# Two last stages of a transformer kernel: attention's work spread over its steps, and mixture-of-experts in one block with rounded output products

## What is computed

```python
h = layernorm(x) * (1 + ca) + sa
x = x + ga * attention(h)       # 16 heads of 64, all 1024 keys, scores + rel_bias[j - i]
h = layernorm(x) * (1 + cb) + sb
logits = h @ gate_w             # 8 experts
top_w = softmax(two largest logits);  cw = top_w at their experts, 0 elsewhere
for e in range(8):
    out += cw[:, e:e+1] * (gelu(h @ w1[e] + b1[e]) @ w2[e] + b2[e])   # 128 -> 512 -> 128
x = x + gb * out
```

## Time and profile before

| | us |
|---|---|
| median of 3 runs (2817.11 to 2831.84) | 2823.53 |
| the profiled execution | 2821.27 |
| its span, first to last instruction | 2819.3 |

### The profile page before, as it was taken

One profiled execution on the slowest core, in us unless ns is written; L12 is line 12 of the kernel. 1 busy time (PEld: TensorE's weight loads), 2 busy tenths in 40 slices (PEclk: granted clock), 3 DMA queues, 4 the chain that ended last, 5 costly groups with the idle time before them and its releaser, 6 DMA issues. The chain is left out here.

```text
span 2819.3 us, 119352 instructions
## 1 busy us (share of the span) xinstructions
PE 2504.6 (89%) x52916; PEld 2026.4 (72%) x53012; DVE 2073.4 (74%) x2409; ACT 1931.1 (68%) x3809; POOL 1455.5 (52%) x1016
## 2 busy tenths in 40 slices
PE   4469999999999999999999998589999999986998
PEld 2157877777888788787878887366676676765887
DVE  5378888778888888887878885489888888973112
ACT  2367888788888888888888876566666666643443
POOL 0188887778788878877888774112122121211000
PEclk8689999999999999999999999799999999997999
DMA  0223433333333333333433332122223132210000
GB/s 33 61 68 91 98 95 83 83 94 84 95 92 96 83 94 88 100 79 91 98 88 77 90 77 53 44 48 59 61 47 71 38 70 59 47 34 16 16 22 30
DMA packets 274599, 193.96 MB, mean 69 GB/s; under 512 B 117545, under 2 KB 215857, under 8 KB 273969
## 3 DMA queue, kind: packets, MB, share of 16 engines
q1 hardware_dynamic: 274096, 186.49, 27.3%
HBM read 29.10 MB, written 1.05 MB: 11 GB/s over the span
## 5 line engine op out<-in xcount | busy, mean ns | idle before, releaser
L728 POOL TENSOR_TENSOR lt_t_sin<-lt_qk,lt_tab 128x512 f32<-128x512 f32 x384 | 685.6, 1807 | 263.1 <-DVE lt_qk L1097 260.6
L733 POOL TENSOR_TENSOR lt_qr<-lt_qr,lt_t_sin 128x1024 f32<-128x1024 f32 x192 | 455.5, 2372 | 27.9 <-POOL lt_t_sin L728 0.5
L1631 DVE TENSOR_REDUCE fa_neg_max<-bank 128x1 f32<-128x1024 f32 x256 | 301.2, 1218 | 91.2 <-PE bank L1458 90.9
L1090 DVE TENSOR_REDUCE lt_ssq<-lt_qr 128x32 f32<-128x2048 f32 x96 | 219.5, 2286 | 155.6 <-ACT lt_qr L962 155.6
L788 PE MATMUL bank<-lt_w_high,lt_x_high 128*128 128x512 f32 x576 | 281.2, 488 | 33.8 <-POOL lt_w_low L696 29.0
L1571 ACT ACTIVATE fa_prob<-bank,fa_neg_max 128x1024 f32<-128x1024 f32 x128 | 142.5, 1113 | 243.7 <-DVE fa_neg_max L1631 127.0
L1641 DVE STREAM_TRANSPOSE fa_prob_t<-fa_prob 128x1024 f32<-128x1024 f32 x256 | 301.8, 1218 | 0.0
L1481 PE MATMUL bank<-fa_prob_t,fa_v 32*64 32x128 f32 x16384 | 276.8, 274 | 23.7 <-issue 17.9
L1481 PEld LDWEIGHTS bank<-fa_prob_t,fa_v 32*64 32x64 f32 x16384 | 240.4, 130 | 71.5 <-issue 43.2
L805 PE MATMUL bank<-ident,lt_qr 128*128 128x128 f32 x1536 | 234.5, 276 | 32.3 <-POOL lt_qr L733 15.9
L1097 DVE TENSOR_TENSOR lt_qk<-lt_qk,lt_rn 128x2048 f32<-128x2048 f32 x96 | 233.0, 2427 | 31.9 <-ACT lt_rn L975 30.7
(11 more groups left out here) (226 smaller groups left out, 5707.1 us busy)
## 6 DMA issues: line engine op xcount, KB each, us to landing
lt_v<-lt_v_tok SPq DMA_DIRECT2D x576, 128.0 KB
fa_v<-fa_v_tok SPq DMA_DIRECT2D x256, 128.0 KB, 3.1
lt_v<-lt_v_tok SPq DMA_DIRECT2D x192, 64.0 KB
lt_k_t<-lt_k_t SPq DMA_DIRECT2D x84, 128.0 KB, 2.6
lt_v<-lt_v SPq DMA_DIRECT2D x168, 64.0 KB, 2.0
lt_w_raw<-in_lt_wqkv_dram SPq DMA_DIRECT2D x36, 256.0 KB, 3.8
lt_x_s<-h_in SPq DMA_DIRECT2D x96, 64.0 KB, 2.7
lt_f_x<-h_mid SPq DMA_DIRECT2D x96, 64.0 KB, 2.1
```

Of the source, the lines that this page charges most:

```text
L728: pool.tensor_tensor(dst[:, :, i, :], src[:, :, 1 - i, :], tab[:, g // 2 % 2, 1, at:at + 32].unsqueeze(1).to_broadcast([P, HEADS, 32]), AL ...
L733: pool.tensor_tensor(qr[:, g % 2, half], qr[:, g % 2, half], t_sin[:, :], ALU.add).then_inc(S.rotated, 1)
L1631: dve.tensor_reduce(neg_max[:, u % 2, par:par + 1], bank[:, 2 * par:2 * par + 2, :].rearrange("p a n -> p (a n)"), AX.X, ALU.max, negate=T ...
```

## The change

In `full_attention`: the jobs come two at a time, at s=0, 2 and 3 (their banks are renumbered). The result of a quad is copied by ScalarE (`att`) at s=3, and Gpsimd multiplies it by the inverses (`divide`), where VectorE did both. The bias band is split by ScalarE (`round_rel`) and Gpsimd (`split_rel`) into `rel_high` and `rel_low`, `anti` is rounded once, and four rounded matmuls take the place of two full ones. `load_rel` waits for the remainder of the pair before. Each DMA of `place_v` waits for a further exponential.

In `experts`: one block without a loop holds all. `down` has the hidden features of the result on partitions and 512 tokens in the row, and is made in three rounded products from `w2_high`, `w2_low`, `hid_high` and `hid_low`. ScalarE rounds hidden blocks 0 and 2, VectorE 1 and 3, and VectorE makes all differences. The routing weights are turned by PE (`turn_weights`, banks 6 and 7), copied by ScalarE behind the Gelus of the second chunk, stored as 8 rows to HBM (`cw_kept`) and read back, one row per expert over all partitions (`spread_weights`, 1 MB each). `weigh` adds the bias (a column of the transposed `b2`), multiplies, and adds to `acc`, for 512 tokens at once. PE takes the logits and the transpose of `b2` first, then `up(0)`; VectorE takes the remainders of `h`, the routing, and then the hidden blocks. Weights of expert e are loaded once expert e-2 has passed its Gelus, and split behind the second chunk of expert e-1. At the end VectorE multiplies by `gb` and adds `x_main` for each chunk, PE turns it (`turn_out`, four full float32 transposes), ScalarE copies it out, SP stores it.

```diff
--- before.py
+++ after.py
...
         def jobs_at(u):
             q, s = u // UPQ, u % UPQ
             half = q // QPH + 1
-            if s % 2 == 1 or half >= HALVES:
+            if s == 1 or half >= HALVES:
                 return []
-            first = JPH * half + 6 * (q % QPH)
-            return list(range(first, first + 4) if s == 0 else range(first + 4, first + 6))
+            first = JPH * half + 6 * (q % QPH) + max(0, 2 * (s - 1))
+            return [first, first + 1]
...
                         for a in range(4):
+                            exponents = 3 * (QB * half - 1) + 4 * i + a
+                            if exponents > 0:
+                                sp.wait_ge(S.probs, exponents)
...
+                def divide(q):
+                    pool.wait_ge(S.att, q + 1)
+                    if q >= 2:
+                        pool.wait_ge(S.out, 2 * (q - 1))
+                    pool.tensor_tensor(att_t[:, q % 2, :].rearrange("p (u a r) -> p a u r", u=UPQ, a=4),
+                                       att[:, :, :].rearrange("p a (u r) -> p a u r", u=UPQ),
+                                       inv_all[:, :, :].rearrange("p a (u r) -> p a u r", u=UPQ),
+                                       ALU.mult).then_inc(S.att_t, 1)
...
+                    if u % UPQ == 3 and weighed_at(u) is not None:
+                        divide(weighed_at(u))
                     for j in jobs_at(u):
                         if j % JPH in LOWS:
                             make_low(j)
+                    if u % PER == 3 and u // PER < PAIRS:
+                        split_rel(u // PER)
...
-                                pe.wait_ge(S.rel, 4 * (u // PER + 1))
-                                pe.wait_ge(S.load, 16)
+                                pe.wait_ge(S.rel_low, u // PER + 1)
+                                pe.wait_ge(S.anti, 1)
                             cols = slice(P, 2 * P) if qb == 6 else slice(0, 2 * P)
-                            for par in range(2):
-                                mm = pe.matmul(bank[:, 2 * par, 0:P * (qb - 5)], anti[:, :], rel[:, par, cols],
-                                               start=False, stop=True)
+                            for n, r in enumerate((rel_high, rel_low)):
+                                for par in range(2):
+                                    mm = pe.matmul(bank[:, 2 * par, 0:P * (qb - 5)], anti[:, :], r[:, par, cols],
+                                                   start=False, stop=n == 1)
...
-                    if s == 2:
+                    if s >= 2:
...
+                def empty_att(q):
+                    if q >= 1:
+                        act.wait_ge(S.att_t, q)
+                    act.copy(att[:, :, :], bank[:, 4:8, 0:P]).then_inc(S.att, 1)
+
+                def round_rel(p):
+                    act.wait_ge(S.rel, 4 * (p + 1))
+                    if p >= 1:
+                        act.wait_ge(S.scores, PER * p)
+                    act.copy(rel_high[:, :, :], rel[:, :, :]).then_inc(S.rel_high, 1)
...
+                    if u % UPQ == 3 and weighed_at(u) is not None:
+                        empty_att(weighed_at(u))
...
+                    if u == 2:
+                        act.wait_ge(S.load, 16)
+                        act.copy(anti[:, :], anti_in[:, :]).then_inc(S.anti, 1)
+                    if u % PER == 3 and u // PER < PAIRS:
+                        round_rel(u // PER)
...
+                def spread_weights(e):
+
+                    if e >= 2:
+                        sp.wait_ge(S.part, NCH * (e - 1))
+                    sp.dma_start(cw_all[:, e % 2, :, :].rearrange("p c n -> p (c n)"),
+                                 cw_kept[e:e + 1, :].to_broadcast([P, TOK])).then_inc(s_cw[e % 2], 16)
...
+                sp.wait_ge(S.cw_t, NCH)
+                sp.dma_start(cw_kept, cw_t[:, :]).then_inc(S.cw_kept, 16)
+                sp.wait_ge(S.cw_kept, 16)
+                spread_weights(0)
+                spread_weights(1)
+                for e in range(2, EXPERTS):
+                    load_expert(e)
+                    spread_weights(e)
...
+                def down(n):
+                    e = n // NCH
+                    if n % NCH == 0:
+                        pe.wait_ge(S.w_low, 2 * e + 2)
+                    if n >= 2:
+                        pe.wait_ge(S.part, n - 1)
+                    o = bank[:, DOWN[n % 2], :]
+                    for j in range(EFB):
+                        pe.wait_ge((S.high_even, S.high_odd)[j % 2], EFB // 2 * n + j // 2 + 1)
+                        pe.matmul(o, w2_high[:, e % 2, j, :], hid_high[:, n % 2, j, :], start=j == 0, stop=False)
+                        pe.matmul(o, w2_low[:, e % 2, j, :], hid_high[:, n % 2, j, :], start=False, stop=False)
+                        pe.wait_ge(S.hid_low, EFB * n + j + 1)
+                        mm = pe.matmul(o, w2_high[:, e % 2, j, :], hid_low[:, n % 2, j, :], start=False, stop=j == EFB - 1)
+                    mm.then_inc(S.down, 1)
+
+                def turn_weights():
+                    pe.wait_ge(S.cw, 1)
+                    pe.wait_ge(S.b2_out, 1)
+                    for c in range(NCH):
+                        if c >= 2:
+                            pe.wait_ge(S.cw_t, c - 1)
+                        for i in range(4):
+                            mm = pe.transpose(bank[0:EXPERTS, 6 + c % 2, i * P:(i + 1) * P], cw[:, 4 * c + i, :], ident[:, :])
+                        mm.then_inc(S.cw_turned, 1)
...
+                up(0)
+                for n in range(CHUNKS):
+                    if n + 1 < CHUNKS:
+                        up(n + 1)
+                    if n == 0:
+                        turn_weights()
+                    down(n)
+                    if n == CHUNKS - 1:
+                        for c in range(NCH):
+                            turn_out(c)
...
+                def gelu(n):
+                    e, c = n // NCH, n % NCH
+                    if c == 0:
+                        act.wait_ge(s_b1[e % 2], 16 * (e // 2 + 1))
+                    for j in range(EFB):
+                        act.wait_ge(S.up, EFB * n + j + 1)
+                        if n >= 2:
+                            act.wait_ge(S.hid_low, EFB * (n - 2) + j + 1)
+                        act.activation(hid[:, n % 2, j, :], bank[:, UP[j], :], ACT.Gelu, bias=b1[:, e % 2, j:j + 1])\
+                           .then_inc(S.gelu, 1)
+                        if j % 2 == 0:
+                            act.wait_ge(S.gelu, EFB * n + j + 1)
+                            if n >= 2:
+                                act.wait_ge(S.down, n - 1)
+                            act.copy(hid_high[:, n % 2, j, :], hid[:, n % 2, j, :]).then_inc(S.high_even, 1)
...
+                for n in range(CHUNKS):
+                    gelu(n)
+                    if n == 1:
+                        for c in range(NCH):
+                            act.wait_ge(S.cw_turned, c + 1)
+                            act.copy(cw_t[:, c * CH:(c + 1) * CH], bank[0:EXPERTS, 6 + c % 2, :]).then_inc(S.cw_t, 1)
+                        split_high(1)
+                    elif n % NCH == 1 and n // NCH + 1 < EXPERTS:
+                        split_high(n // NCH + 1)
+                for c in range(NCH):
+                    empty_turned(c)
...
+                def split_hidden(n):
+
+                    for j in range(EFB):
+                        if n >= 2 and j == 0:
+                            dve.wait_ge(S.down, n - 1)
+                        if j % 2 == 0:
+                            dve.wait_ge(S.high_even, EFB // 2 * n + j // 2 + 1)
+                        else:
+                            dve.wait_ge(S.gelu, EFB * n + j + 1)
+                            dve.tensor_copy(hid_high[:, n % 2, j, :], hid[:, n % 2, j, :]).then_inc(S.high_odd, 1)
+                            dve.wait_ge(S.high_odd, EFB // 2 * n + j // 2 + 1)
+                        dve.tensor_tensor(hid_low[:, n % 2, j, :], hid[:, n % 2, j, :], hid_high[:, n % 2, j, :].bitcast(F32),
+                                          ALU.subtract).then_inc(S.hid_low, 1)
+
+                def weigh(n):
+
+                    e, c = n // NCH, n % NCH
+                    if c == 0:
+                        dve.wait_ge(s_cw[e % 2], 16 * (e // 2 + 1))
+                    if n == 0:
+                        dve.wait_ge(S.b2_out, 1)
+                    if n > NCH:
+                        dve.wait_ge(S.added, n - NCH)
+                    dve.wait_ge(S.down, n + 1)
+                    dve.scalar_tensor_tensor(out=acc[:, c, :] if e == 0 else part[:, :], in0=bank[:, DOWN[n % 2], :],
+                                             scalar=b2[:, e:e + 1], in1=cw_all[:, e % 2, c, :], op0=ALU.add, op1=ALU.mult)\
+                       .then_inc(S.part, 1)
+                    if e > 0:
+                        dve.wait_ge(S.part, n + 1)
```

(19 more changed lines are left out.)

423 lines of the change are left out of this document (159 added, 264 removed).

## The result

| | before | changed |
|---|---|---|
| median of the runs, us | 2822.9 | 2753.6 (2746.4 to 2760.7) |
| ratio, 95% interval | | 0.9756 (0.9735 to 0.9777) |
| profiled execution, its span | 2821.3, 2819.3 | 2760.7, 2758.9 |
| maxima, first to 128th start | 709.6 | 695.2 |
| experts, block's start to the end | 255.8 | 203.7 |

What follows compares the result with a forecast made beforehand. PE bounds the experts' loop; attention's ordinary step is a loop through three engines. Attention -35 us (2.3 a half, x16 = 37, less 1.6 at the end) and experts -50 take 2821.3 to 2736 us; own range 2717 to 2754.

Steps and rivals of the forecast that it cites:

- (e): Experts' output products: twelve rounded matmuls replace 16 full-precision ones, a chunk falls from 6.33 to 5.5 us; -26.6 us.
- (f): Experts' cover: ScalarE at 4.7 and VectorE at 4.8 us a chunk stay under PE's 5.5, so PE stays the bound.
- (g): Experts without barriers: PE's idling between pairs of experts and other time beyond 32x6.33 goes; -13.8 us.
- (h): Experts' start: routing beside the first expert brings the first product 18.7 us earlier; +11 (6 to 18) comes back.
- (i): Experts' tail, last product to end: 9.0 us instead of 11.2; -2.2 us.
- (a): Attention projections: two jobs at s=0, 2 and 3 remove the long step; about 1.6 us a half.
- (c): Attention bias product in rounded form: the two bias steps' extra falls from 0.9 and 1.17 to 0.75 and 0.7 us.
- (b): Attention division by row sums leaves VectorE: 0.25 us a half back, but +1.6 us at the very end.
- R1: Rival: attention does not speed up, ScalarE's copy and strict order delaying the exponentials; 2771 us, chance 0.12.
- R2: Rival: experts stay at 6.3 us a chunk, bound by VectorE or the Gelu-rounding-difference chain; 2762 us, chance 0.11.
- R3: Rival: weight loads don't hide behind the experts' rounded output matmuls, +75 us; 2811 us, chance 0.01.
- R4: Rival: spreading one HBM row over 128 partitions is far slower than other loads, kernel slower; up to 3240 us, chance 0.02.

Runs made afterwards that it cites:

- e11: Changed kernel without the second rounded product (low weights against high hidden values) of the experts' output; ratio 0.9728, 2748.5 us.
- e2: Changed kernel with the old distribution of projections: four behind a group's first step, two behind the third, none behind the fourth; ratio 0.9769, 2758.5 us.
- e12: Changed kernel with the attention's bias products in two full float32 products instead of four rounded ones; ratio 0.9792, 2769.0 us.
- e10: Changed kernel with the attention's division on VectorE again, in the first step behind the group; ratio 0.9809, 2774.9 us.
- e9: Changed kernel with second and third steps' 128 value products cut in two, projections or output product between; ratios 0.9738 and 0.9745, first median 2752.0 us.
- e7: Changed kernel with each projection from the third half on multiplying only 32 columns, instruction count unchanged; ratio 0.9767, 2762.1 us.
- e1: Changed kernel with the 16 value-placing transfers of a half no longer waiting for exponentials; ratio 0.9761, 2758.3 us.

## Why the prediction was right, and where it was off

The likeliest case came true in the experts and in part in the attention. 2753.6 is at the upper edge of the forecast's own 2717 to 2754. The experts' sum was right for the reasons given; the attention gave 13 of its 35 us. That the total is still inside is luck: the lower bound allowed for a wait of 0.1 in each unit and for dear bias products, neither of which happened, and the time was lost in stops that the prediction does not name.

- **(e)** 5.60 a chunk for 5.5: the products stand 0.233 us apart, 24 x 0.233, where I had 2.75 for twelve against the 2.84 of the earlier trace rows. **(f)** held: VectorE is next, at 4.72 (e11) for 4.8. From start to start a difference took 0.60 as forecast, a cast 0.46 (0.49), the bias and weight 0.78 (0.75), the addition 0.61 (0.70).
- **(g)** No break between experts is left. **(h)** First product 8.7 us behind the block's start for 28.2 before, 19.5 for the 18.7 forecast. What comes back: from 2563.94 to 2578.76 PE makes the first 36 products and the turns, 14.8 us where 36 products at 0.233 take 8.4, so 6.4 (11 forecast). The first twelve take 5.3 of it, at a granted clock of 0.50; around the turns and behind them it is 0.98 and 1.00, so PE ran cold ahead of the turns and not behind them. PE waits 1.85 before the last turns, not 5. The spreading of the weights (1 MB in 4.4 us, and 4.3 to 6.6 for the others; 7 forecast) holds up VectorE's first weighing for 7.1 us, but not PE, whose chunks follow each other at 5.60 from then on. **(i)** 9.2 us from the last product to the end, 9.0 forecast. Together: 19.5 at the start, 30.6 from the first product to the end of the last (216.4 to 185.8; 29.4 forecast), 2.0 at the end, 52 for 50. In the middle two errors nearly cancel: the shorter chunks bring 23.4 for 26.6, and 6.4 comes back for 11.
- **(a)** was mis-sized in clean steps, 1.1 a half by e2 for 1.6, and (c) gave 0.45 by e12 for 0.62. What is left for (b) is 0.7 for 0.25, by difference alone; e10 only bounds it. That the sum of 2.3 a half came out right is luck. **The step that failed is "x16" and the bound beside it, "the jitter of the mean (5.60 against 5.48) goes too, another 10".** The mean of 5.60 (5.59 by the first maxima alone) lay over the clean half's 5.48, some 4 of the 9 us behind gaps in PE's instruction stream and the rest unexplained, and I had not looked at what that jitter was. It did not go: it grew from 9 to 30 us, since the evening took from PE the room that hid most of the gaps (back to 11 us with the old jobs, e2). "no step is heavier than one that costs 5.0 now" is true of the work and says nothing of a stop.
- The end of the attention took 4.5 more in the first profile, where 1.6 were forecast, and 1.8 in the second. From the last maximum to the experts' first product the granted clock is 0.75 in the first, 0.85 in the second and 0.87 before, so that part varies.
- **R1** is half of what happened, the attention giving 13 us of 35, for another reason than it names: in every step of units 8 to 127 the exponential starts within 0.1 us of the end of its maximum, so none waits for the copy. **R2, R3, R4** did not happen. On R3: twelve output products a chunk took 2.80, 0.233 from one to the next, with a full-height weight load of 0.19 ahead of each, which therefore costs nothing. By the rule of the Trainium skill's "TensorE: Matmul & The Clock Gate", Part 3, each would be paid; the trace disagrees here too.

## What to carry to other kernels

Evening the work of an engine between steps pays only down to what hides its stops: before levelling, compare the mean of a step with its clean value and find out what the difference is. Long runs of short instructions (here 256 in 2.1 us) are where PE's instruction fetch shows; putting longer multiplications in the middle of the run won 4 to 9 us here (e9), and room behind it hides a stop as far as the room goes (e2, and 0.5 us a gap in e7). Count the stops before crediting a difference of a few us to an edit: the changed kernel's own profiles differ in 5 of 23, and moving the stream by 64 instructions put all of them elsewhere, at 1 to 4 us in sum.

## What was not expected of the hardware

- PE stops at borders of 256 instructions, two products' starts 0.5 to 1.9 us apart in the changed kernel (up to 2.7 in e1), mostly at the same unit and product in each execution; it goes on 1.2 to 1.8 us after a 16 KB packet of the instruction queue has ended. With 64 instructions put ahead the borders fall 32 products earlier.
- Two stops of 1.31 and 1.89 us, some 4 us of work apart, were followed by 10.2 us at half the clock (e7); 0.89 and 1.60 in the same place by 3.5 us (changed kernel, second profile).
- VectorE's cast of 128x512 to the rounded form: 0.42 us alone, 1.50 beside GpSimd's two-operand work (e11).

Not tried: moving the borders to places where a long multiplication stands, which would show what the stops cost in all; the order of before with the attention's other parts one by one, and the experts' routing and barriers by themselves; for these the traces alone speak.
